# A selective-scan loop on one Trainium2 core: its order of work shifted by a few units, and the multiply by C done for two units at once

## The chip, the core and the metric

The kernel runs on one core of one Trainium2 chip. The core has five engines that run their own instruction streams and meet at semaphores: TensorE (PE; its weight loads are shown apart as PEld), VectorE (DVE), ScalarE (ACT), GpSimd (POOL) and SyncE (SP, which here issues the DMAs). The metric is the device time of one launch, in microseconds. The kernel before took 1730.82 us in the median of 3 runs (1728.37 to 1734.09).

## What is computed

Two attention and mixture-of-experts blocks stand ahead of and beside a stack of four Mamba layers; the change lies in the Mamba stack alone. For each of 4 layers and each of 4 parts of the batch (512 token columns in the kernel's layout), the reference does:

```python
xz = jnp.einsum('bld,ed->ble', x, in_w)
xi, z = jnp.split(xz, 2, axis=-1)
xc = silu(causal depthwise conv of 4 taps (xi) + cb)
dbc = jnp.einsum('bld,ed->ble', xc, xp_w)
dt, Bm, Cm = jnp.split(dbc, [DT_RANK, DT_RANK + D_STATE], axis=-1)
delta = jax.nn.softplus(jnp.einsum('blr,dr->bld', dt, dtw) + dtb)
A = -jnp.exp(A_log)
h = exp(delta * A) * h + (delta * u) * B        # the scan over the tokens
y = sum over the 16 states of h * C, + u * D
y = y * silu(z)
x = jnp.einsum('bld,od->blo', y, ow)
```

256 channels times 16 states give 4096 rows of a scan over the tokens, for each batch part. All of it is float32.

## The kernel before, in words

The Mamba stack is one block (from line 1333 on) whose engines each carry their own loop. The outermost loop runs over 4 layers `l`, inside it 4 steps `b`, one for each batch part. A step has 32 **units** (`UN`), numbered p: 128 scan rows each (32 channels times 4 states). Every fourth unit (p = 3, 7, 11, ...) is of kind DIRECT, the others are "main" units of three state groups k = 0, 1, 2, with eight units g = 0 to 7 in each group; so k = 0 fills p = 0 to 9, k = 1 p = 10 to 20, k = 2 p = 21 to 30.

For a unit the engines do this, each in its own turn:

- PE (`input_of`, lines 1638 to 1651) puts the scan's input into one of three PSUM banks `dbx`: four transposes of `scaled` for a main unit (L1650), one matmul with `spread` for a DIRECT unit (L1647). With three banks, unit p waits until the scan of unit p-3 has ended.
- ACT (`decay`, L1810) makes exp(dt * A) into a ring of five buffers (`DR`). The ring starts again with unit 0 in buffer 0 although 32 is no multiple of 5, so that unit 0 of a step needs the scan of unit 30, and unit 1 the scan of unit 31.
- DVE (`scan`, L1918) runs the scan into `hs`, a ring of eight (`HR`). For a DIRECT unit it first multiplies the bank by B (`times_b`, L1908).
- POOL (`weigh`, L1535) multiplies `hs` by C into `hcm` (ring of eight) or, for DIRECT units, `hck` (ring of four).
- PE (`fold_quad`, L1667) sums four such products into `y_bank`, eight times in a step, each time when the fourth of them is there.

Between the units each engine does the rest of the step, partly for the next one, n = b+1, at places that the code fixes by the unit's number (v for PE, w for ACT, u for DVE, p for POOL). PE: `z` at v = 0 and 2, `x_proj` at 3, `turn_b` at 6, `dt_proj` at 7 and 8, `start_y` at 10 and 11, `turn_du` at 18 and 19, `out_proj` of the step before at 22 (both halves), and `xi`, the convolution as four shifted matmuls for each half of the channels, with two taps at each of v = 24, 25, 27 and 28 (L1585). ACT: after the decay of unit 0 `silu_xi`, `silu_z` and two loads of function tables (L1737, L1743, L1821); then `copy_dbc`, `copy_bt`, `abs_and_relu` and `softplus`, `scale_by_b` for the groups 2 and 0, `copy_dut` in two halves, `copy_out`. DVE: `gate_y` after u = 4, `make_dt` and `make_du` after u = 12 to 15, and in layer 0 `mix` after u = 9. POOL: `scale_by_b` for group 1 (16 instructions a step: three after each of p = 27 to 31 and one after p = 0), in step b = 2 four `make_tap`, and in the steps 1 and 2 of layer 0 eight gathers by indirect DMA. SP stores and reads back the rows of B, C (`spread_direct`, `spread_c`) and dt (`spread_dt`), always in the same order.

The PSUM banks `slot` 0, 1 and 2 are shared by these side jobs (xi, z, x_proj, the transposes, dt, duT, out), so that each waits until the last reader of its bank is through. Ahead of the first step a prologue does the same jobs once for batch part 0, and `xi` for part 1. The four places where the order stands on PE are these lines of `step`:

```python
if v == 22:
    out_proj(l, b - 1)
...
if v in (24, 25, 27, 28):
    xi(l, b + 2, (v - 24) // 3, (0, 1) if v in (24, 27) else (2, 3))
```

## Time and profile before

| what | value |
|---|---|
| median of 3 runs | 1730.82 us (1728.37 to 1734.09) |
| the profiled execution | 1734.24 us, its span 1732.5 us |
| busy, of the span | PE 1307.1 us (75%), DVE 1186.3 (68%), ACT 1059.3 (61%), POOL 1006.6 (58%) |
| the Mamba stack | from about 748 us to 1716 us of the span |
| first scan of it starts, last ends | 787.9 us, 1703.5 us |

The page sums over the whole launch; the stretch of the Mamba stack is read in windows and in the timeline, engine by engine. "[4.42 <-ACT decay L1810]" behind an instruction says that its engine stood idle for 4.42 us before it and what ended that. An x4 behind a row merges four instructions that follow one another; a float32 matmul counts as two. Instructions of one engine overlap a little at their ends, so their pitch (start to start) is shorter than their duration, and it is the pitch that a sum of times needs.

### The profile page before, as it was taken

How to read it: one execution, taken by the hardware profiler on the slowest of the kernel's cores; microseconds unless marked ns; L12 is line 12 of the kernel's file. 1: busy time of each engine (PE TensorE's matmuls, PEld its weight loads, DVE VectorE, ACT ScalarE, POOL GpSimd, SP SyncE). 2: the span in 40 equal slices, each digit the busy share in tenths (PEclk: the TensorE clock that was granted, in tenths of full speed). 3: DMA queues.
4: the chain of work that ended last, by engine and by line, in shares of the span. 5: the costliest groups of instructions: out<-in, count | busy, mean ns of one | idle time of the engine just before them, and what ended most of it. 6: DMA issues, size and time to landing. Idle time of an engine off the chain costs nothing. (4 is left out here: it accounts for less than half of the span.)

```text
span 1732.5 us, 23857 instructions
## 1 busy us (share of the span) xinstructions
PE 1307.1 (75%) x6419; PEld 641.4 (37%) x6419; DVE 1186.3 (68%) x1664; ACT 1059.3 (61%) x1846; POOL 1006.6 (58%) x1092
## 2 busy tenths in 40 slices
PE   5213388898931799967977888898888989898884
PEld 2113033333431455633433334343443434343431
DVE  4786367686766422215888788878888778877884
ACT  2210378797811122346877779877798778777782
POOL 1642310110152530054988978898899888888894
PEclk9655589998965799987998999999999999999998
DMA  1110231321201301442332234313341233323331
GB/s 53 37 37 11 91 109 64 100 79 61 91 26 39 134 12 33 122 108 76 75 79 71 48 73 112 79 38 83 87 112 52 62 77 94 82 55 78 87 92 54
DMA packets 86612, 124.39 MB, mean 72 GB/s; under 512 B 16946, under 2 KB 43440, under 8 KB 86112
## 3 DMA queue, kind: packets, MB, share of 16 engines
q1 hardware_dynamic: 79680, 104.65, 23.0%
q0 software_dynamic: 6816, 18.42, 3.5%
q8 instruction: 44, 0.72, 0.2%
q14 instruction: 72, 0.59, 0.1%
HBM read 100.27 MB, written 24.31 MB: 72 GB/s over the span
## 5 line engine op out<-in xcount | busy, mean ns | idle before, releaser
L1918 DVE TENSOR_TENSOR_SCAN hs<-decay,dbx 128x512 f32<-128x512 f32 x512 | 592.3, 1203 | 100.7 <-ACT decay L1810 91.5
L1535 POOL TENSOR_TENSOR hcm<-hs,Cc 128x512 f32<-128x512 f32 x384 | 488.8, 1286 | 110.3 <-DVE hs L1918 106.8
L1810 ACT ACTIVATE decay<-dtr,a_cur 128x512 f32<-128x512 f32 x512 | 355.6, 714 | 145.3 <-DVE hs L1918 136.4
L1650 PE MATMUL dbx<-ident_sb,scaled 128*128 128x128 f32 x1536 | 242.5, 289 | 98.6 <-DVE hs L1918 95.2
L1650 PEld LDWEIGHTS dbx<-ident_sb,scaled 128*128 128x128 f32 x1536 | 176.5, 145 | 314.3 <-DVE hs L1918 240.5
L1790 ACT ACTIVATE scaled<-duT,BT 128x256 f32<-128x256 f32 x528 | 236.0, 497 | 0.1
L1535 POOL TENSOR_TENSOR hck<-hs,Cc 128x512 f32<-128x512 f32 x128 | 168.0, 1312 | 19.1 <-PE y_bank L1667 11.8
L1647 PE MATMUL dbx<-du,spread_sb 128*128 128x512 f32 x256 | 154.9, 690 | 11.0 <-DVE hs L1918 11.0
L1908 DVE TENSOR_TENSOR dbx<-dbx,Bb 128x512 f32<-128x512 f32 x128 | 88.6, 692 | 78.4 <-PE dbx L1647 77.3
L1585 PE MATMUL slot<-XT,w_tap 128*128 128x512 f32 (+3 forms) x288 | 138.4, 608 | 4.5 <-PEq L1063 3.7
L758 ACT ACTIVATE ex<-tt 128x1024 f32<-128x1024 f32 x128 | 136.8, 1069 | 4.2 <-DVE tt L843 3.5
L1517 POOL TENSOR_SCALAR scaled<-duT,BT 128x256 f32<-128x256 f32 x271 | 125.9, 480 | 8.7 <-PE dbx L1650 7.9
L1667 PE MATMUL y_bank<-hcm,fold_sb 128*32 128x512 f32 x768 | 108.0, 636 | 12.2 <-POOL hcm L1535 12.2
L842 DVE TENSOR_TENSOR tt<-bank_l,gt 128x512 f32<-128x512 f32 x128 | 87.6, 685 | 38.1 <-PE bank_l L667 34.5
L752 ACT ACTIVATE gt<-bank_d,dgh 128x512 f32<-128x512 f32 x128 | 89.0, 699 | 28.8 <-PE bank_d L661 28.8
L600 POOL CAST weight_rows<-w_row 128x1 uint32 (+1 forms) x26 | 4.9, 188 | 168.8 <-PE bank_e L685 168.8
L843 DVE SCALAR_TENSOR_TENSOR tt<-bank_l,gt 128x512 f32<-128x512 f32 x128 | 87.2, 681 | 0.0
L699 PE MATMUL bank_pv<-ex,v_head 128*32 128x512 f32 x512 | 76.0, 675 | 2.6 <-DVE ybig L832 2.6
L1502 POOL MEMSET w_dt<- 40x256 f32 x1 | 0.3, 306 | 124.5 <-POOLq L1063 124.5
L1585 PEld LDWEIGHTS slot<-XT,w_tap 128*128 128x128 f32 x288 | 52.3, 196 | 52.5 <-issue 52.5
L1647 PEld LDWEIGHTS dbx<-du,spread_sb 128*128 128x128 f32 x256 | 44.2, 205 | 63.5 <-DVE hs L1918 46.6
L661 PE MATMUL bank_d<-q_stack,k_stack 112*128 112x512 bf16 x128 | 54.3, 429 | 12.4 <-DMA k_stack<-qk_parts 7.8
(320 smaller groups left out, 2055.9 us busy)
## 6 DMA issues: line engine op xcount, KB each, us to landing
dtr<-dt_turn SPq DMA_DIRECT2D x68, 512.0 KB, 8.4
Cc<-bc_turn SPq DMA_DIRECT2D x268, 64.0 KB, 2.1
dt_turn<-dt SPq DMA_DIRECT2D x17, 512.0 KB, 2.8
Bb<-bc_turn SPq DMA_DIRECT2D x68, 64.0 KB, 2.1
conv_row<-in_conv_row SPq DMA_DIRECT2D x5, 512.0 KB, 3.8
w_rg<-in_w_rg SPq DMA_DIRECT2D x8, 256.0 KB, 2.8
w_ru<-in_w_ru SPq DMA_DIRECT2D x8, 256.0 KB, 3.0
w_rd<-in_w_rd SPq DMA_DIRECT2D x8, 256.0 KB, 3.9
```

The lines of the kernel that those rows point to most:

```text
L752: nc.scalar.activation(gt[:, st % RING, :], bank_d[st % 2][:, :], ACT.Tanh, scale=dgh[:, st // 16:st // 16 + 1]).then_inc(s_G, 1)
L758: nc.scalar.activation(ex[:, (st // 4) % 2, st % 4, :, :], tt[:, st % RING, :, :], ACT.Exp).then_inc(s_E, 1)
L1517: nc.gpsimd.tensor_scalar(scaled[:, (n + 1) % 2, kk, :, j, :], duT[:, n % 2, kk, :].rearrange("p (g c) -> p g c", c=32), BT[:, n % 2, kk, ...
L1535: nc.gpsimd.tensor_tensor(dst, hs[:, p % HR, :], rows, ALU.mult).then_inc(s_hc, 1)
L1585: last = mm(slot[h][:, d:512], w_tap[:, 3 - d, P * h:P * h + P], XT[:, n % 4, 0:512 - d], start=(d == 0), stop=(d == 3))
L1647: mm(dbx[p % 3][:, :], spread[:, g % 4, :], du[:, b % 2, g // 4, :], start=True, stop=True).then_inc(s_bx, 1)
L1650: last = nc.tensor.transpose(dbx[p % 3][:, P * kk:P * kk + P], scaled[:, (b + k) % 2, kk, g, :, :].rearrange("p j c -> p (j c)"), ident[:, :])
L1667: last = mm(y_bank[h][32 * q:32 * q + 32, :], fold[:, :], src, start=False, stop=((k, h) in ((DIRECT - 1, 0), (DIRECT, 1))), tile_position ...
L1790: nc.scalar.activation(scaled[:, (n + k) % 2, kk, :, j, :], duT[:, n % 2, kk, :].rearrange("p (g c) -> p g c", c=32), ACT.Copy, scale=BT[: ...
L1810: nc.scalar.activation(dec[:, p % DR, :], dtr[:, b % 2, g, :], ACT.Exp, scale=a_cur[:, 4 * g + k:4 * g + k + 1]).then_inc(s_dec, 1)
L1908: TT(dbx[p % 3][:, :], dbx[p % 3][:, :], Bb[:, b % 2, :], ALU.mult).then_inc(s_mul, 1)
L1918: nc.vector.tensor_tensor_scan(hs[:, p % HR, :], dec[:, p % DR, :], dbx[p % 3][:, :], 0.0, ALU.mult, ALU.add).then_inc(s_sc, 1)
```

## The change

- **POOL, C.** Main units are weighed in pairs of one state group (g = 0 and 1, 2 and 3, ...) in one instruction of 1024 columns, issued at the second unit's place; the C row is read twice by a broadcast. DIRECT units are weighed alone as before. A scan that reuses an `hs` buffer now waits for the pair (`hc_after`).
- **POOL, B.** The 16 `scale_by_b` go from three after each of p = 27 to 31 to two after each of p = 28 to 31 and 0 to 3.
- **DVE.** `times_b` of a DIRECT unit stands right before the scan of that unit (u % 4 == 3), not one scan earlier. `gate_y` moves from u = 4 to 7.
- **PE.** `xi` is cut into single taps at v = 19, 22, 23, 24 and 25, 27, 28, 29. `out_proj` moves from 22 to 13 and 14, one half each; `x_proj` is one half at 3 and one at 4; `z` comes at 0 and 1 in the other order of halves; `turn_du` from 18, 19 to 16, 17; the last two folds of the step before from 4, 5 to 5, 7; `dt_proj` from 7, 8 to 8, 9.
- **ACT.** `silu_z`, Abs and `copy_dut` each work on two banks in one instruction of 1024 columns (the `slot` banks become one tensor). The bias of dt comes in by a 41st row of `w_dt` against a row of ones in `dbc`; Relu falls away, and DVE's `make_dt` takes max(x, 0) in its addition. `scale_by_b` of group 2 goes to w = 13 to 20, that of group 0 starts at 22; `copy_out` moves from 25 to 16.
- **Prologue.** `xi` of part 1 goes to the `y_bank` banks and, with its Silu and the z of part 0, stands ahead of the first step; half of the first 16 `scale_by_b` of group 0 are DVE's, and POOL does 8 of its own ahead of the first step; SP sends dt out ahead of the three C rows.

The core of the diff (semaphore counts that only follow from it are left out):

```diff
-            slot = [st5.enter_context(nc.psum_tensor(f"slot{i}", [P, 512], fp32)) for i in range(3)]
+            slots = st5.enter_context(nc.psum_tensor("slots", [P, 3, 512], fp32))
+            slot = [slots[:, i, :] for i in range(3)]
...
+            weighed = lambda k, g: hc_after[place[k, g]]
+            hc_after = {}
+            for p, (k, g) in enumerate(units):
+                if k == DIRECT:
+                    hc_after[p] = p + 1
+                elif g % 2 == 1:
+                    hc_after[p] = hc_after[place[k, g - 1]] = p + 1
...
+                        sp.dma_start(w_dt[40:41, :].rearrange("o (h p) -> o h p", p=P), one(A["pre_cols"])[:, :, 2:4].rearrange("o p h -> o h p"), allow_slow_non_contiguous=True).then_inc(s_wpre, 16)
...
@@ -1524,15 +1533,15 @@
                             wait(pool, s_fk, at(l, b, 2, g // 4))
                             if g == 0:
                                 pool.wait_ge(s_c3[b % 2], by_parity(l, b, 128))
-                            dst, rows = hck[:, g % KR, :], Cc[:, 3 + b % 2, :]
+                            nc.gpsimd.tensor_tensor(hck[:, g % KR, :], hs[:, p % HR, :], Cc[:, 3 + b % 2, :], ALU.mult).then_inc(s_hc, 1)
                         else:
-                            m = order_in_main[k, g]
-                            if m % 4 == 0:
+                            m, q = order_in_main[k, g], place[k, g - 1]
+                            if m % 4 == 1:
                                 wait(pool, s_fm, at(l, b, 6, m // 4 - 1))
-                            if g == 0:
+                            if g == 1:
                                 pool.wait_ge(s_cb[k], at(l, b, 64, 64))
-                            dst, rows = hcm[:, m % MR, :], Cc[:, k, :]
-                        nc.gpsimd.tensor_tensor(dst, hs[:, p % HR, :], rows, ALU.mult).then_inc(s_hc, 1)
+                            nc.gpsimd.tensor_tensor(hcm[:, (m - 1) % MR:m % MR + 1, :], hs[:, q % HR:p % HR + 1:p - q, :],
+                                                    Cc[:, k:k + 1, :].broadcast_to([P, 2, 512]), ALU.mult).then_inc(s_hc, 2)
...
-                            weigh(l, b, p)
-                            if p == 0:
-                                scale_by_b(l, b, 15)
-                            if p >= 27:
-                                for x in range(3 * (p - 27), 3 * (p - 27) + 3):
+                            if units[p][0] == DIRECT or units[p][1] % 2 == 1:
+                                weigh(l, b, p)
+                            if p < 4:
+                                for x in (8 + 2 * p, 9 + 2 * p):
+                                    scale_by_b(l, b, x)
+                            if p >= 28:
+                                for x in (2 * (p - 28), 2 * (p - 28) + 1):
                                     scale_by_b(l, b + 1, x)
...
-                            if v == 0:
-                                z(l, b, 0)
-                            if v == 2:
-                                z(l, b, 1)
-                            if v == 3:
-                                x_proj(l, n)
-                            if not first(l, b):
-                                if v == 4:
-                                    fold_quad(l, b - 1, 2, 1)
-                                if v == 5:
-                                    fold_quad(l, b - 1, DIRECT, 1)
-                                if v == 22:
-                                    out_proj(l, b - 1)
+                            if v in (0, 1) and not first(l, b):
+                                z(l, b, 1 - v)
+                            if v in (3, 4):
+                                x_proj(l, n, v - 3)
                             if v == 6:
                                 turn_b(l, n)
-                            if v in (7, 8):
-                                dt_proj(l, n, v - 7)
+                            if v in (8, 9):
+                                dt_proj(l, n, v - 8)
+                            if not first(l, b):
+                                if v == 5:
+                                    fold_quad(l, b - 1, 2, 1)
+                                if v == 7:
+                                    fold_quad(l, b - 1, DIRECT, 1)
+                                if v in (13, 14):
+                                    out_proj(l, b - 1, v - 13)
                             if v in (10, 11):
                                 start_y(l, b, v - 10)
                             if v == 12:
                                 fold_quad(l, b, 0, 0)
                             if v == 15:
                                 fold_quad(l, b, 0, 1)
-                            if v in (18, 19):
-                                turn_du(l, n, v - 18)
+                            if v in (16, 17):
+                                turn_du(l, n, v - 16)
                             if v == 20:
                                 fold_quad(l, b, 1, 0)
                             if v == 21:
                                 fold_quad(l, b, DIRECT, 0)
-                            if v in (24, 25, 27, 28):
-                                xi(l, b + 2, (v - 24) // 3, (0, 1) if v in (24, 27) else (2, 3))
+                            if v in (19, 22, 23, 24):
+                                tap = (19, 22, 23, 24).index(v)
+                                xi(l, b + 2, 0, (tap,))
+                            if v in (25, 27, 28, 29):
+                                tap = (25, 27, 28, 29).index(v)
+                                xi(l, b + 2, 1, (tap,))
                             if v == 26:
                                 fold_quad(l, b, 1, 1)
                             if v == 31:
                                 fold_quad(l, b, 2, 0)
...
-                    x_proj(0, 0)
+                        xi(0, 0, h, every)
...
                         dt_proj(0, 0, h)
...
-                    for h in range(2):
-                        xi(0, 1, h, (0, 1, 2, 3))
+                    xi(0, 1, 1, every, y_bank)
+                    for h in (1, 0):
+                        z(0, 0, h)
...
                         wait(act, s_op, at(l, b, 1, -1))
-                        for h in range(2):
-                            act.wait_ge(s_z, at(l, b, 2, h + 1))
-                            nc.scalar.activation(zs[:, b % 2, h, :], slot[2 if h == 0 else 0][:, :], ACT.Silu).then_inc(s_zs, 1)
+                        act.wait_ge(s_z, at(l, b, 2, 2))
+                        nc.scalar.activation(zs[:, b % 2, :, :], slots[:, 0:3:2, :], ACT.Silu).then_inc(s_zs, 1)
...
+                        nc.scalar.activation(dt[:, :, :], slots[:, 0:2, :], ACT.Abs).then_inc(s_ab, 1)
+
+                    def exp_dt(l, n):
+                        act.wait_ge(s_ab, at(l, n, 2, 1))
                         nc.scalar.activation(dt[:, :, :], dt[:, :, :], ACT.Exp, scale=-1.0).then_inc(s_ab, 1)
...
-                            if w == 0:
+                            if w == 0 and not first(l, b):
                                 silu_xi(l, n)
                                 silu_z(l, b)
...
-                            if w == 8:
+                            if w == 7:
                                 copy_bt(l, n)
-                            if w in (10, 11):
-                                abs_and_relu(l, n, w - 10)
+                            if w == 10:
+                                abs_dt(l, n)
+                            if w == 11:
+                                exp_dt(l, n)
                             if w == 12:
-                                softplus(l, n)
-                            if 14 <= w < 22:
-                                for x in (2 * (w - 14), 2 * (w - 14) + 1):
+                                log_dt(l, n)
+                            if w in last_scales:
+                                for x in last_scales[w]:
                                     scale_by_b(l, b, 2, x)
-                            if w in (21, 22):
-                                copy_dut(l, n, w - 21)
-                            if 23 <= w < 31:
-                                for x in (2 * (w - 23), 2 * (w - 23) + 1):
+                            if w == 16 and not first(l, b):
+                                copy_out(l, b - 1)
+                            if w == 19:
+                                copy_dut(l, n)
+                            if 22 <= w < 30:
+                                for x in (2 * (w - 22), 2 * (w - 22) + 1):
                                     scale_by_b(l, n, 0, x)
-                            if w == 25 and not first(l, b):
-                                copy_out(l, b - 1)
-
+
...
+                    copy_dut(0, 0)
+                    for x in range(8):
                         scale_by_b(0, 0, 0, x)
+                    silu_xi(0, 1, y_bank)
+                    silu_z(0, 0)
+                    act.preload_act_table_set("natural_log_exp_and_others")
...
                 def _(dve):
+                    nc.vector.memset(dbc[32:41, :], 1.0).then_inc(s_one, 1)
...
-                        TT(dt[:, h, :], slot[h][:, :], dt[:, h, :], ALU.add).then_inc(s_dt, 1)
+                        nc.vector.scalar_tensor_tensor(dt[:, h, :], slot[h][:, :], 0.0, dt[:, h, :], ALU.max, ALU.add).then_inc(s_dt, 1)
...
-                        wait(dve, s_hc, at(l, b, UN, p - HR + 1))
+                        wait(dve, s_hc, at(l, b, UN, hc_after[p - HR] if p >= HR else hc_after[p - HR + UN] - UN))
...
-                            if u % 4 == 2:
+                            if u % 4 == 3:
                                 times_b(l, b, u // 4)
                             scan(l, b, u)
-                            if u == 4 and not first(l, b):
+                            if u == 7 and not first(l, b):
...
+                    dve.wait_ge(s_dut, 1)
+                    for x in range(8, 16):
+                        nc.vector.tensor_scalar(scaled[:, 0, x // 4, :, x % 4, :], duT[:, 0, x // 4, :].rearrange("p (g c) -> p g c", c=32),
+                                                BT[:, 0, x // 4, x % 4:x % 4 + 1], 1.0, ALU.mult, ALU.mult).then_inc(s_k[0], 1)
```

Three places as the instruction streams show them. First PE in step 1 of layer 0, around the end of the out projection and the first taps; `dbx` banks are inputs of units, `slot` the side jobs (L1650 and L1647 inputs, L1585 taps, L1667 folds, L1635 the out projection). Before, from v = 22 to 25:

```order
L1650 MATMUL dbx1<-ident_sb,scaled 128x128 x4
L1635 MATMUL slot2<-zs,w_out 128x512 x2
L1647 MATMUL dbx2<-du,spread_sb 128x512
L1650 MATMUL dbx0<-ident_sb,scaled 128x128 x4
L1585 MATMUL slot0<-XT,w_tap 128x512
L1585 MATMUL slot0<-XT,w_tap 128x511
L1650 MATMUL dbx1<-ident_sb,scaled 128x128 x4
L1585 MATMUL slot0<-XT,w_tap 128x510
L1585 MATMUL slot0<-XT,w_tap 128x509
```

The same place now, v = 22 to 25 (L1663 and L1660 inputs, L1597 taps):

```order
L1663 MATMUL dbx1<-ident_sb,scaled 128x128 x4
L1597 MATMUL slots<-XT,w_tap 128x511
L1660 MATMUL dbx2<-du,spread_sb 128x512
L1597 MATMUL slots<-XT,w_tap 128x510
L1663 MATMUL dbx0<-ident_sb,scaled 128x128 x4
L1597 MATMUL slots<-XT,w_tap 128x509
L1663 MATMUL dbx1<-ident_sb,scaled 128x128 x4
L1597 MATMUL slots<-XT,w_tap 128x512
```

Between two inputs there is now one tap where there were two, or the whole out projection; the first tap (512 columns) has gone ahead to v = 19, and the out projection to 13 and 14.

DVE in the same step, from unit 17 on. Before, and now:

```order
L1918 SCALAR_TENSOR_TENSOR hs<-decay,dbx 128x512 x2
L1908 TENSOR_TENSOR dbx<-dbx,Bb 128x512
L1918 SCALAR_TENSOR_TENSOR hs<-decay,dbx 128x512 x4
L1908 TENSOR_TENSOR dbx<-dbx,Bb 128x512
L1918 SCALAR_TENSOR_TENSOR hs<-decay,dbx 128x512 x4
```

```order
L1940 SCALAR_TENSOR_TENSOR hs<-decay,dbx 128x512 x3
L1930 TENSOR_TENSOR dbx<-dbx,Bb 128x512
L1940 SCALAR_TENSOR_TENSOR hs<-decay,dbx 128x512 x4
L1930 TENSOR_TENSOR dbx<-dbx,Bb 128x512
L1940 SCALAR_TENSOR_TENSOR hs<-decay,dbx 128x512 x4
```

The multiply by B follows one scan later, and the scan right behind it is now the one that reads its result.

POOL over the border of two steps. Before, from p = 27 to p = 2 of the next step:

```order
L1535 TENSOR_TENSOR hck<-hs,Cc 128x512
L1517 TENSOR_SCALAR scaled<-duT,BT 128x8x32 x3
L1535 TENSOR_TENSOR hcm<-hs,Cc 128x512
L1517 TENSOR_SCALAR scaled<-duT,BT 128x8x32
L1535 TENSOR_TENSOR hcm<-hs,Cc 128x512 x2
```

Now, from p = 26 to p = 4 of the next step:

```order
L1543 TENSOR_TENSOR hcm<-hs,Cc 128x1024
L1526 TENSOR_SCALAR scaled<-duT,BT 128x8x32 x4
L1543 TENSOR_TENSOR hcm<-hs,Cc 128x1024
L1526 TENSOR_SCALAR scaled<-duT,BT 128x8x32 x2
L1536 TENSOR_TENSOR hck<-hs,Cc 128x512
L1526 TENSOR_SCALAR scaled<-duT,BT 128x8x32 x4
L1543 TENSOR_TENSOR hcm<-hs,Cc 128x1024
L1526 TENSOR_SCALAR scaled<-duT,BT 128x8x32 x4
```

The 16 scalings are spread over eight units instead of six, and a step has 12 products of 1024 columns and 8 of 512 where it had 32 of 512.

## Rows read from the trace of the kernel before

**Rows 1.** Windows, 1414:1471: length, busy PE, PEld, DVE, ACT, POOL, PE clock, DMA, GB/s.

```profile
1414.00:1471.00 57.00, 50.95 (x243) 23.09 (x242) 45.01 (x47) 45.93 (x84) 48.60 (x49) 0.94 0.30 73
```

**Rows 2.** Timeline, ACT: first table load of the steps 4 and 15.

```profile
1033.94 1.28 ACT L1737 ACT_TABLE_LOAD   x1
...
1648.94 1.28 ACT L1737 ACT_TABLE_LOAD   x1
```

**Rows 3.** Waits of DVE from 1072 to 1700 us: total us, times, longest.

```profile
DVE dbx L1908 <- PE dbx L1647: 60.2, 46, 2.9
DVE hs L1918 <- ACT decay L1810: 49.8, 14, 5.5
```

**Rows 4.** Timeline, ACT: a step's border, and Exp of 1024 columns (start, duration).

```profile
1422.12 0.72 ACT L1810 ACTIVATE decay<-dtr,a_cur 128x512 f32<-128x512 f32 x1 [4.87 <-DVE hs L1918]
...
1424.16 1.27 ACT L1737 ACTIVATE xc<-slot,pre_cols 128x512 f32<-128x512 f32 x2
...
1426.68 1.28 ACT L1821 ACT_TABLE_LOAD   x1
...
1441.02 1.05 ACT L1773 ACTIVATE dt<-dt 128x1024 f32<-128x1024 f32 x1
```

**Rows 5.** Timeline, DVE, one step.

```profile
1428.73 1.22 DVE L1918 TENSOR_TENSOR_SCAN hs<-decay,dbx 128x512 f32<-128x512 f32 x1 [4.42 <-ACT decay L1810]
...
1464.01 0.70 DVE L1908 TENSOR_TENSOR dbx<-dbx,Bb 128x512 f32<-128x512 f32 x1 [2.88 <-PE dbx L1647]
1464.62 4.54 DVE L1918 TENSOR_TENSOR_SCAN hs<-decay,dbx 128x512 f32<-128x512 f32 x4
1470.80 0.70 DVE L1908 TENSOR_TENSOR dbx<-dbx,Bb 128x512 f32<-128x512 f32 x1 [1.64 <-PE dbx L1647]
```

**Rows 6.** Timeline, PE: a fold at either clock, the out projection, an input, taps.

```profile
1441.72 1.06 PE L1659 MATMUL y_bank<-xc,d_diag 128*32 128x512 f32 x8
...
1457.07 1.94 PE L1667 MATMUL y_bank<-hcm,fold_sb 128*32 128x512 f32 x8
...
1461.23 1.88 PE L1635 MATMUL slot<-zs,w_out 128*128 128x512 f32 x4
1462.95 1.02 PE L1647 MATMUL dbx<-du,spread_sb 128*128 128x512 f32 x2
...
1465.97 0.60 PE L1650 MATMUL dbx<-ident_sb,scaled 128*128 128x128 f32 x4
1466.40 1.87 PE L1585 MATMUL slot<-XT,w_tap 128*128 128x510 f32 x4
```

**Rows 7.** Timeline, DVE, last stage: L1977 reads what L1974 wrote.

```profile
1722.58 0.68 DVE L1974 TENSOR_TENSOR GATE<-s_bank,GATE 128x512 f32<-128x512 f32 x1
...
1723.30 0.69 DVE L1977 TENSOR_TENSOR X<-X,GATE 128x512 f32<-128x512 f32 x1
```

**Rows 8.** POOL by form (count, busy us, mean ns), and L334 under a busy DVE.

```profile
L1535 POOL TENSOR_TENSOR hcm<-hs,Cc 128x512 f32<-128x512 f32 x384 | 488.8, 1286 | 110.3 <-DVE hs L1918 106.8 <-PE y_bank L1667 2.8
...
L1541 POOL TENSOR_TENSOR w_tap<-w_in,conv_row 128x256 f32<-128x256 f32 x16 | 11.7, 730 | 0.0
...
54.48 2.87 POOL L334 TENSOR_TENSOR sq<-qkv 128x1024 f32<-128x1024 f32 x1
```

**Rows 9.** Timeline, POOL: a product and three scalings.

```profile
1426.24 1.27 POOL L1535 TENSOR_TENSOR hcm<-hs,Cc 128x512 f32<-128x512 f32 x1
1427.48 1.40 POOL L1517 TENSOR_SCALAR scaled<-duT,BT 128x256 f32<-128x256 f32 x3
```

**Rows 10.** Timeline, prologue: the dt rows' way out and back, and the first scans.

```profile
771.55 0.39 SPq L1448 DMA_DIRECT2D dt_turn<-dt  x1
...
787.13 0.72 ACT L1810 ACTIVATE decay<-dtr,a_cur 128x512 f32<-128x512 f32 x1 [8.61 <-DMA dtr<-dt_turn]
...
794.68 1.22 DVE L1918 TENSOR_TENSOR_SCAN hs<-decay,dbx 128x512 f32<-128x512 f32 x1 [5.58 <-ACT decay L1810]
```

**Rows 11.** Timeline, DVE: the last gate, after the last scan.

```profile
1712.45 1.29 DVE L1890 TENSOR_TENSOR zs<-y_bank,zs 128x512 f32<-128x512 f32 x2 [8.90 <-issue]
```

153 lines of the change are left out of this document (75 added, 78 removed).

## The prediction, made before the changed kernel had run

> **What bounds the kernel now.** The launch is one long chain of stages; only the Mamba stack changes, and it holds 968 of the 1732.5 us. So I read windows first. In 57 us of its later layers no engine is full by the page's measure: PE 51.0 us, POOL 48.6, ACT 45.9, DVE 45.0 [rows 1]. When all are near 80 to 90% and none is full, the time goes where they wait for each other, and the next view is the waits of DVE, since its scans are the one thing that cannot be reordered.
>
> A step's length I take from ACT's first table load, once a step: steps 4 to 15 are (1648.94 - 1033.94)/11 = 55.9 us apart [rows 2]; the four of layer 0, with `mix` and the gathers, are longer. From 1072 to 1700 us, 11.2 steps, DVE waited 60.2 us for PE's L1647, always in the multiply by B of a DIRECT unit, and 49.8 us for `decay`: 5.4 and 4.45 us a step [rows 3]. So of 55.9 us DVE works about 46.0 (smaller idle times counted in).
>
> The timeline says what these two are. (a) At a step's border ACT makes the decay of unit 0 only when scan 30 has freed its buffer (1422.12), then loads a table, does four Silus, loads the other table, and comes to the decay of unit 1 at 1427.96 [rows 4]; DVE has run dry and stands 4.42 us [rows 5]. (b) The bank of a DIRECT unit p may be filled once scan p-3 has ended; its matmul takes 1.02 to 1.12 us and DVE wants it after one scan of 1.13 us (the pitch: 4.54/4). There is no slack, and anything that PE puts between two inputs shows. It puts the whole out projection ahead of unit 23: DVE waits 2.88 us. Taps by twos around 24 to 28: 1.64 us [rows 5, 6].
>
> **PE's budget** decides what (b) is worth. Four units take DVE 4 x 1.13 + 0.61 = 5.1 us. PE's four inputs take 3 x 0.45 to 0.6 + 1.0, about 2.5 us, so 2.6 us are left for side jobs in each group of four. A fold or `start_y` costs 1.0 us of pitch, a tap or half an out projection 0.86 (1.72 for the out projection, 1461.23 to 1462.95, and two taps show the same 1.87 as it does) [rows 6]. In v = 20 to 27 the kernel before has three folds, the out projection and six taps: 3.0 + 1.7 + 5.2 = 9.9 us against 5.2. The excess of 4.7 us is the 2.88 + 1.64 seen. The method reproduces the trace there.
>
> **The change, part by part** (times a step of layers 1 to 3 unless said).
>
> *Taps, out projection, multiply by B.* Now v = 20 to 27 hold three folds and five taps, 7.3 us against 5.2; the 2.1 us excess meets a new slack of one scan, 1.1 us, since the multiply by B comes one scan later, and the groups ahead (16 to 19: two `turn_du` and one tap, some 2.1 us) leave PE no debt. In v = 4 to 15 PE has about 11.5 us of side jobs against 7.8, but there DVE itself does six extra operations (two each of `gate_y`, `make_dt`, `make_du`, at 0.58, 3.5 us). I leave 0.6 us of waits out of 5.4: -4.8 us. PE's whole work does not shrink; at these pitches its 32 inputs and side jobs come to about 46.5 us, so it fits into 52, with little to spare.
>
> *The price of the later multiply.* The scan now reads what the instruction just ahead wrote. No row of the stack shows that. In the last stage a TT that depends on its predecessor starts 0.72 us after it [rows 7]; in the stack the scan behind a multiply that it does not need starts 0.61 us after it [rows 5]: +0.11 us, eight times, +0.9. Bounds: 0 (if the scan starts late anyway) to 0.2 each, 0 to 1.6 us. The Trainium skill (VectorE: DVE Perf Modes, "The DRAIN you can't avoid") says that a semaphore between Vector operations costs nothing extra; by it this term would be 0. The last-stage pair speaks against that, so I keep 0.9.
>
> *The border.* It stays, and gets a little longer. z of half 0 must wait for the first Silu of xi (it takes bank 0), which ends about 2.73 us after unit 0's decay began; its matmul takes 1.02. Before, ACT did one z Silu meanwhile; now a single one of 1024 columns starts after it and takes about as long as ACT's Exp of 1024 columns, 1.05 us. So the second table load starts some 4.9 us after the decay instead of 4.56 [rows 4]: +0.4.
>
> *ACT elsewhere.* Relu gone, Abs and `copy_dut` merged: about 2 us less work, on an engine on which DVE waited elsewhere for under 0.5 us a step. I cost it at nothing; the cover is the decay ring, five deep. `copy_dbc` and Abs come later because PE's `x_proj` and `dt_proj` do, by one unit; the ring carries that too.
>
> *POOL.* A product takes 1.27 us, pitch 1.24; three scalings 1.40, pitch 1.36 [rows 9]. The 1024-column product is not in the trace with these operands. 256 columns of the same kind take 0.73 us and 512 take 1.286, so 0.556 for 256 more, and 1024 would take 1.286 + 2 x 0.556 = 2.4 us. A 1024-column product of an earlier stage, beside a DVE at work on two SBUF operands, took 2.87 [rows 8]. Bounds 2.3 and 2.9; I take 2.4, since the scans beside it read one operand from PSUM and the 512-column rows there are at their low value. POOL's step is then 12 x 2.36 + 8 x 1.24 + 16 x 0.455 = 45.5 us where it was 47.0; at 2.87 it is 51.5. POOL waits about 1 us for the fold of the first four DIRECT products, which stays at v = 21. So POOL is no bound in layers 1 to 3. The pair is finished later than its first half was, but a scan reuses its buffer only eight units on. Worth: nothing there. In layer 0, steps 1 and 2 have 8 gathers of about 1.3 us on POOL and step 2 the four taps: 45.5 + 10.4 + 2.9 = 59 us where it was 60.3; there it counts.
>
> *Sum of a step*: -4.8 + 0.9 + 0.4 = -3.5, and with the 0.4 us of small waits for decay and issue that taking the load off ACT and PE should remove, -3.9: 52.0 us. Twelve steps: **-47 us**. Layer 0 I give -3 a step, as POOL and `mix` hold part of it: **-12**.
>
> *Prologue.* dt goes out to DRAM at 771.55 because SP is still issuing C rows, and the first decay waits until 787.13 for the way back [rows 10]. Now SP sends it as soon as it is made, near 767.7: -3.8. Silu, z and both table loads are done while the rows travel, so that the 5.58 us hole after scan 0 [rows 10] is gone. Against this, a load of 256 single elements for the bias row joins the first weights: 0 to 1 us, taken as 0.2. Sum **-9**. If C rows in the same queues slow the dt rows, 3 us of it go.
>
> *End.* From the last scan's end, 1703.55, to the last gate DVE waits 8.90 us for POOL and the folds [rows 11]; POOL has then five triples of scalings between products, now four pairs, and two pairs ahead of the last product: about 7 x 0.45, less half a product for the pairing: **-2.5**.
>
> Sum: 47 + 12 + 9 + 2.5 = 70.5 us off the profiled execution's own 1734.2 us: 1664. The profiled execution lies 3.4 us above the median of the runs, 1730.8, so for a median I say **1660 us**. About 0.3%, 5 us, is what a measurement of this kernel can tell from no change.
>
> **Rivals.**
> 1. *PE becomes the bound by its clock.* The granted clock in these 57 us is 0.94 of full [rows 1]: near 1457 a fold takes 1.94 us instead of 1.06 [rows 6], so the engine is at the 1.2 GHz level there, after a stretch in which it had waited for `du`. The new order moves `turn_du` two units earlier, ahead of the second `du`, which puts a wait of some 1.4 us at v = 17. The missing 6% are 6.8 us at half clock, 3.4 us of work lost. If that stays, and falls where PE has no slack, more than half of it shows, 2 us a step: 54: layers 1 to 3 give -23, layer 0 -6, ends -11, total -40: 1691. For: PE has only 5 us to spare. Against: PE stands idle less than before. Chance 0.22.
> 2. *Better than the sum*: the scan behind the multiply costs nothing extra (the rule named above), and the low-clock stretch vanishes with PE's idle time, so that no wait for PE is left. Then 0.9 + 0.6 more a step, 16 steps, 24 us: 1636. The rule alone gives 1646. Chance 0.13.
> 3. *The waits only move.* PE's excess in v = 4 to 15 shows on DVE, say 1.3 us in each group, and the border grows by 1: a step gains nothing, only prologue and end count: 1719. Chance 0.06.
> 4. *Slower: POOL's pairs are dear.* If a 1024-column product with a strided `hs` pair and a broadcast C row runs at a slower rate than a plain one, POOL becomes the bound, and DVE waits for `hs` buffers. POOL's step without pairs is 9.9 + 7.3 + 1.0 = 18.2 us; it reaches 55.9 at 3.14 us a pair, and from there the kernel is slower. At 3.5 us a step is 60.2: 16 x 4.3 - 11 = 58 us more: 1789. For: no row has this form. Against: a broadcast operand is in nearly all forms that a plain one is, and even the row under contention is 2.87. Chance 0.03.
>
> **How the numbers follow.** The forecast has 0.56, and its own range, from the bounds of the dependence (0 to 1.6 us), the pair and the prologue, is 1646 to 1680. The range reaches to rival 1 and to rival 2: 1636 to 1694; it leaves out rivals 3 and 4 and their neighbours, about one in ten, and as much again for what I have not seen. Faster by over 0.3%: the forecast, rivals 1 and 2 and nearly all of 3, 0.93. Slower: rival 4 and an unseen wait, 0.04. The same: 0.03.
>
> **What would show it.** Steps 52 us apart at ACT's table load. DVE's waits for L1660 (the old L1647) near zero, its wait for decay once a step and 4.5 to 5 us. Multiply to scan 0.72 us apart at the eight DIRECT units. POOL's 1024-column rows at 2.4 us. Scan 0 starting near 784 us and scan 1 right behind. If POOL's pairs are over 2.9 us, or DVE's waits for `hs` buffers appear, the POOL part is wrong; if waits for PE stay above 2 us a step, the PE budget or its clock is; if the hole at the border is under 4 us, I have misread what unit 1's decay waits for.

## The result: 0.6% faster, and 60 us short of the forecast

| | before | after |
|---|---|---|
| median | 1729.85 us (20 runs) | 1719.98 us (1701.73 to 1736.61, 20 runs) |
| ratio | | 0.9941 (95%: 0.9923 to 0.9959) |
| profiled execution, its span | 1734.24, 1732.5 us | 1714.21, 1712.4 us |
| DVE busy, whole launch | 1186.3 us | 1226.5 us |
| POOL busy, whole launch | 1006.6 us | 975.4 us |

The forecast was 1660 us with a range of 1636 to 1694, so 1720 lies outside it, though it is faster, as was forecast. The two profiled executions differ by 20 us, the medians by 10: single runs of this kernel scatter by a per cent. To see where the 20 us lie I cut each launch at ACT's first table load of a step, as [rows 2] did:

| piece of the span, us | before | after | forecast |
|---|---|---|---|
| to the border load of step 1 | 847.13 | 837.62 (-9.5) | -9, and -3 for step 0 |
| steps 1 to 3 (layer 0) | 186.81 | 189.30 (+2.5) | -9 |
| steps 4 to 14, a step | 55.91 | 54.42 (-16.4 in all) | 52.0 (-43) |
| the last step and the end | 83.56 | 86.84 (+3.3) | -6.4 |

The prologue with the first step came within 3 us of the forecast. The other steps did not. ACT's first table load in steps 4 and 15 of the kernel after (start, duration, engine, line):

```profile
1026.92 1.28 ACT L1757 ACT_TABLE_LOAD   x1
...
1625.56 1.28 ACT L1757 ACT_TABLE_LOAD   x1
```

**The waits fell, most of the way.** DVE's waits from 1060 to 1680 us (11.4 steps) in the kernel after: total us, times, longest.

```profile
DVE hs L1940 <- ACT decay L1827: 43.3, 12, 4.2
DVE dbx L1930 <- PE dbx L1660: 17.1, 29, 0.8
DVE hs L1940 <- PE dbx L1663: 6.1, 11, 2.1
DVE hs L1940 <- issue: 3.7, 6, 1.9
DVE hs L1940 <- POOL hcm L1543: 2.4, 7, 0.4
```

The wait at the multiply by B fell from 5.4 us a step [rows 3] to 1.5, the border's is 3.8. All waits together are 6.4 us a step where they were some 10 and where the forecast came to about 5. Yet a step is only 1.5 us shorter, so DVE's own work must have grown, and the windows say so. The stretch of [rows 1] in the kernel after:

```profile
1414.00:1471.00 57.00, 48.45 (x245) 21.62 (x245) 48.86 (x48) 46.60 (x84) 49.70 (x43) 1.00 0.35 89
```

DVE is busy for 48.9 us there and was for 45.0 (part of that is that 57 us now hold more of a step: a whole one, from table load to table load, has 47.2 us at 1409.87 and had 44.8 at 1422.86). PE's granted clock is full in this stretch; it isn't in others, as e4 will show. The groups of DVE's instructions tell which ones grew (x count, busy us, mean ns), first of before, then of after, 760 to 1720 us:

```profile
L1883 DVE TENSOR_TENSOR du<-dt,xc 128x512 f32<-128x512 f32 x34 | 32.8, 966 | 0.0
L1897 DVE SCALAR_TENSOR_TENSOR GATE<-back,share,GATE 128x128 f32<-128x128 f32 x32 | 23.7, 802 | 0.1
```

```profile
L1905 DVE TENSOR_TENSOR du<-dt,xc 128x512 f32<-128x512 f32 x34 | 52.6, 1550 | 0.0
L1919 DVE SCALAR_TENSOR_TENSOR GATE<-back,share,GATE 128x128 f32<-128x128 f32 x32 | 28.5, 951 | 0.1
```

The same 34 `du`, with the same operands, cost 1550 ns each instead of 966. The timeline shows how. DVE and then POOL in one step of the kernel after:

```profile
1435.60 1.21 DVE L1940 TENSOR_TENSOR_SCAN hs<-decay,dbx 128x512 f32<-128x512 f32 x1
1436.72 2.28 DVE L1905 TENSOR_TENSOR du<-dt,xc 128x512 f32<-128x512 f32 x1
1438.93 0.69 DVE L1930 TENSOR_TENSOR dbx<-dbx,Bb 128x512 f32<-128x512 f32 x1
```

```profile
1434.85 1.29 POOL L1536 TENSOR_TENSOR hck<-hs,Cc 128x512 f32<-128x512 f32 x1
1436.08 5.14 POOL L1543 TENSOR_TENSOR hcm<-hs,Cc 128x1024 f32<-128x1024 f32 x2
1441.19 1.72 POOL L1536 TENSOR_TENSOR hck<-hs,Cc 128x512 f32<-128x512 f32 x1
```

`du` begins 0.64 us after a pair did (the row merges two; at 2.38 us the first ends near 1438.45) and lasts to 1439.00, 0.55 us beyond that pair. In another step it lasts 4.59 us (1107.79 to 1112.38), through two pairs (1107.15 to 1111.83). And with POOL quiet, in the kernel before, DVE and POOL:

```profile
821.90 0.67 DVE L1883 TENSOR_TENSOR du<-dt,xc 128x512 f32<-128x512 f32 x1
```

```profile
822.06 1.63 POOL L1535 TENSOR_TENSOR hcm<-hs,Cc 128x512 f32<-128x512 f32 x1 [1.03 <-DVE hs L1918]
```

There POOL had run dry, `du` was first and took 0.67 us, and it is POOL's product that is stretched, from 1.27 to 1.63 us. The scans and the multiply by B, with one input in SBUF and one in PSUM, show no such thing: beside the same POOL instructions they keep their 1.21 and 0.69 us. Only `du` and `mix` read two SBUF tensors in the loop. With 0.67 us for a free `du` and 0.29 for a free `mix` (found below) the hold makes up 10.0 + 14.4 = 24.4 us of DVE's busy time in the kernel before and 29.8 + 19.2 = 49.0 after: 25 us more, on the engine whose time the forecast had added up.

The Trainium skill (SBUF — State Buffer, "Who interferes with whom") has this rule: a DVE instruction with two SBUF inputs contends with a GpSimd instruction that reads SBUF, whoever issues first gets the shared ports for the whole instruction, and the other fully blocks. The traces agree, with 0.67 against 2.28 us. They show more than it says in one respect, the 4.59 us through two instructions.

### The profile page after: what moved, and what is told of

The parts are those of the page before. It is cut to its first block and busy times, and to the rows that moved or that the text cites. A ratio compares the mean times of both kernels' runs of the same rounds, so it can differ in the third digit from the quotient of the medians.

```text
span 1712.4 us, 23568 instructions
## 1 busy us (share of the span) xinstructions
PE 1307.6 (76%) x6419; PEld 638.9 (37%) x6419; DVE 1226.5 (72%) x1673; ACT 1018.5 (59%) x1754; POOL 975.4 (57%) x893
## 5 line engine op out<-in xcount | busy, mean ns | idle before, releaser
L1543 POOL TENSOR_TENSOR hcm<-hs,Cc 128x1024 f32<-128x1024 f32 x192 | 456.3, 2385 | 31.8 <-DVE hs L1940 27.2
L1827 ACT ACTIVATE decay<-dtr,a_cur 128x512 f32<-128x512 f32 x512 | 350.5, 711 | 69.9 <-DVE hs L1940 66.2
L1663 PEld LDWEIGHTS dbx<-ident_sb,scaled 128*128 128x128 f32 x1536 | 183.8, 147 | 315.3 <-DVE hs L1940 185.9
L1663 PE MATMUL dbx<-ident_sb,scaled 128*128 128x128 f32 x1536 | 253.9, 290 | 55.8 <-DVE hs L1940 54.1
L1807 ACT ACTIVATE scaled<-duT,BT 128x256 f32<-128x256 f32 x520 | 229.4, 496 | 2.0 <-PE dbx L1663 1.9
L1660 PE MATMUL dbx<-du,spread_sb 128*128 128x512 f32 x256 | 146.1, 654 | 8.8 <-DVE hs L1940 8.8
L1597 PE MATMUL slots<-XT,w_tap 128*128 128x512 f32 (+3 forms) x272 | 143.9, 616 | 3.7 <-PEq L1063 3.7
L1526 POOL TENSOR_SCALAR scaled<-duT,BT 128x256 f32<-128x256 f32 x264 | 122.0, 480 | 1.4 <-issue 1.4
L1312 DVE TENSOR_TENSOR hid<-sil,u_bank 128x512 f32<-128x512 f32 x32 | 21.9, 687 | 59.4 <-ACT sil L1222 59.0
L1660 PEld LDWEIGHTS dbx<-du,spread_sb 128*128 128x128 f32 x256 | 43.7, 202 | 55.6 <-issue 27.5
```

The lines of the kernel that those rows point to most:

```text
L1526: nc.gpsimd.tensor_scalar(scaled[:, (n + 1) % 2, kk, :, j, :], duT[:, n % 2, kk, :].rearrange("p (g c) -> p g c", c=32), BT[:, n % 2, kk, ...
L1543: nc.gpsimd.tensor_tensor(hcm[:, (m - 1) % MR:m % MR + 1, :], hs[:, q % HR:p % HR + 1:p - q, :], Cc[:, k:k + 1, :].broadcast_to([P, 2, 512 ...
L1597: last = mm(dst[h][:, d:512], w_tap[:, 3 - d, P * h:P * h + P], XT[:, n % 4, 0:512 - d], start=(d == 0), stop=(d == 3))
L1660: mm(dbx[p % 3][:, :], spread[:, g % 4, :], du[:, b % 2, g // 4, :], start=True, stop=True).then_inc(s_bx, 1)
L1663: last = nc.tensor.transpose(dbx[p % 3][:, P * kk:P * kk + P], scaled[:, (b + k) % 2, kk, g, :, :].rearrange("p j c -> p (j c)"), ident[:, :])
L1807: nc.scalar.activation(scaled[:, (n + k) % 2, kk, :, j, :], duT[:, n % 2, kk, :].rearrange("p (g c) -> p g c", c=32), ACT.Copy, scale=BT[: ...
```

## The experiments

Each was profiled and timed in five rounds beside the kernel before; ratios are to that kernel on the same chip. Theory H is the hold, as read above.

| kernel | median us | ratio, 95% | to step 1 | steps 1-3 | a step of 4-14 | rest |
|---|---|---|---|---|---|---|
| e0_after_again | 1716.4 | 0.9925 (0.9897-0.9954) | 835.6 | 188.2 | 55.18 | 83.9 |
| e1_no_pairs | 1735.3 | 1.0042 (1.0026-1.0059) | 835.8 | 185.5 | 56.55 | 83.8 |
| e2_before_pairs | 1738.8 | 1.0067 (1.0044-1.0090) | 846.6 | 187.8 | 55.97 | 88.1 |
| e3_b_early | 1749.0 | 1.0127 (1.0104-1.0150) | 837.4 | 196.5 | 56.58 | 84.4 |
| e4_du_psum | 1676.9 | 0.9700 (0.9679-0.9721) | 837.2 | 186.5 | 51.87 | 80.5 |
| e5_du_pool | 1735.1 | 0.9865 (0.9837-0.9893) | 863.6 | 191.5 | 53.98 | 85.0 |
| e6_du_gap | 1725.6 | 0.9809 (0.9781-0.9837) | 860.8 | 187.7 | 54.02 | 81.6 |
| e8_pool_mix | 1736.4 | 0.9867 (0.9840-0.9893) | 856.4 | 192.1 | 54.30 | 84.8 |
| e9_fold_early | 1720.5 | 0.9779 (0.9751-0.9808) | 863.9 | 185.3 | 53.54 | 80.6 |
| e10_gap_fold | 1679.1 | 0.9713 (0.9688-0.9739) | 837.5 | 186.2 | 52.00 | 82.6 |
| e11_du_bank | 1696.3 | 0.9806 (0.9780-0.9831) | 840.7 | 187.1 | 53.10 | 83.7 |
| e12_bank_fold | 1696.0 | 0.9807 (0.9786-0.9827) | 839.3 | 184.9 | 52.97 | 83.0 |
| e13_mix_gap | 1667.6 | 0.9645 (0.9621-0.9668) | 833.7 | 178.8 | 52.13 | 82.1 |
| e14_ring_on | 1654.5 | 0.9571 (0.9547-0.9595) | 834.3 | 185.6 | 50.17 | 79.8 |
| e15_ring_mix | 1644.5 | 0.9513 (0.9489-0.9537) | 834.6 | 178.1 | 50.22 | 79.9 |
| e16_mix_quarter | 1671.1 | 0.9673 (0.9647-0.9698) | 832.5 | 181.3 | 51.96 | 80.5 |

The last four columns are of each profiled execution. e5, e6, e8 and e9 ran on a chip where the stages ahead of the stack took some 25 us more (first scan 811.80 in e9 against 785.90) and the kernel before took 1761.5 us; their steps compare, their totals only by the ratio.

### One part alone

**e4_du_psum**: `du` reads the PSUM bank, so its softplus is left out.

```diff
-TT(du[:, n % 2, h, :], dt[:, h, :], xc[:, n % 2, h, :], ALU.mult)
+TT(du[:, n % 2, h, :], slot[h][:, :], xc[:, n % 2, h, :], ALU.mult)
```

> The kernel after, with du's first input read from the PSUM bank (dt before the softplus, which is left out of du) instead of from SBUF: the same shape and cost for DVE, but only one of its inputs lies in SBUF. Theory H: du takes 0.67 us or a little more at all 34 places (busy 23 us in place of 53), and the launch gets up to 30 us shorter: 1690 to 1702. Theory P: du takes 0.67 too, but the waits for PE take the place: 1713 to 1722. Rival to both, that du is slow for another reason than two SBUF inputs: du stays at 1.5 us and the time at 1720.

```profile
L1905 DVE TENSOR_TENSOR du<-slots,xc 128x512 f32<-128x512 f32 x34 | 22.6, 667 | 0.0
```

All 34 take 667 ns, and the launch is about 40 us shorter, more than the 30 of `du` itself: PE's wait for `du` (35.0 us in the kernel after) falls to 11.6. Steps 4 to 14 are 51.87 us apart; the forecast said 52.0. Theory P is out, and so is another reason for the slow `du`: only the place of one input changed.

**e4 also frees PE's clock.** Steps 4 to 14 as one stretch, in the kernel before, in the kernel after and in e4 (us, then busy PE, PEld, DVE, ACT, POOL, the granted clock, DMA):

```profile
1033.94:1648.94 615.00, 540.93 (x2641) 247.77 (x2640) 502.29 (x507) 497.55 (x903) 533.54 (x541) 0.95 0.32 77
1026.92:1625.56 598.64, 535.88 (x2642) 242.15 (x2641) 525.75 (x507) 472.55 (x847) 514.78 (x409) 0.96 0.33 79
1023.70:1594.32 570.62, 522.09 (x2642) 233.29 (x2641) 500.49 (x507) 471.11 (x847) 506.01 (x409) 0.99 0.35 83
```

DVE works 45.7 us a step before, 47.8 after and 45.5 in e4, and the clock rises too. It is uneven from step to step. In the kernel after, five of these eleven steps have the clock at 1.00 throughout and take 52.2 to 53.1 us, from table load to table load; the other six, at 0.91 to 0.97, take 54.0 to 58.6 (two of them also have a `du` of 4.59 us). Two steps with the same place in their layer (b = 2) and the same two `du` (0.87 and 2.22 us), and in each PE at its wait for `du`:

```profile
1136.94:1191.92 54.98, 49.73 (x243) 22.77 (x241) 47.42 (x47) 42.69 (x76) 48.84 (x41) 0.94 0.32 75
1357.63:1409.87 52.24, 46.99 (x243) 21.15 (x241) 46.94 (x47) 42.68 (x76) 48.85 (x41) 1.00 0.34 79
```

```profile
1170.32 1.09 PE L1637 MATMUL slots<-ident_sb,du 128*128 128x128 f32 x4 [2.81 <-DVE du L1905]
1389.49 0.63 PE L1637 MATMUL slots<-ident_sb,du 128*128 128x128 f32 x4 [2.81 <-DVE du L1905]
```

PE had stood for 2.81 us both times. In the first step the granted clock is at its lower level, 0.50, from 1169.9 to 1173.3, and the same transposes take 1.09 us instead of 0.63; with a second such stretch, at 1146.0, behind PE's wait for a scan at the border, that step is 2.7 us longer. Why the clock fell in one and not in the other is open. In steps 4 to 14 of the kernel after ten such stretches last 44 us in all (61 us in the kernel before), five of them at PE's wait for `du` or just behind it; in e4 there are two (7 us) and none at that wait. My estimate from these rows: of the 28 us that e4 saves in steps 4 to 14, some 10 are the shorter `du` at full clock (52.5 us a step against 51.6), and the other 18 lie in the six steps with a low clock. No run keeps the hold and gives the clock back, so the two are not parted further.

**e1_no_pairs**: products by C one unit at a time again, the rest of after stays.

```diff
-if units[p][0] == DIRECT or units[p][1] % 2 == 1:
-    weigh(l, b, p)
+weigh(l, b, p)
```

> The kernel after, with POOL's product by C one unit at a time (512 columns) again; all else stays. Theory H (DVE is held by POOL): a DVE operation with two SBUF inputs (du, and in layer 0 mix) stands while POOL's product runs, and the 2.38 us pairs made that longer: du takes 1550 ns in the mean where it took 966 before and 0.67 when free, and du and mix together lost about 45 us where they had lost 21. With single products du's mean falls below 1.1 us, some 20 us come back, less what POOL itself loses (1.4 us a step, where it is not the bound nothing): 1700 us, 1692 to 1712. Theory P (PE has no time left): DVE's long du only fills time in which PE would be late; du gets shorter, DVE's waits for PE grow by as much, and the time stays at 1715 to 1725.

Missed, and it corrected the theory. `du` got worse, not better:

```profile
L1900 DVE TENSOR_TENSOR du<-dt,xc 128x512 f32<-128x512 f32 x34 | 65.0, 1913 | 0.0
```

DVE's `du` and POOL in one step:

```profile
1442.92 4.06 DVE L1900 TENSOR_TENSOR du<-dt,xc 128x512 f32<-128x512 f32 x1
```

```profile
1442.68 3.75 POOL L1540 TENSOR_TENSOR hcm<-hs,Cc 128x512 f32<-128x512 f32 x3
```

It is held through three products in a row, to 0.55 us after their end. So the length of one instruction isn't what counts, but how far POOL is behind at that moment: with work queued it can go from one instruction to the next without DVE getting in. The pairs save POOL time and so shorten the queue; within the new order they are worth 15 to 19 us.

**e2_before_pairs**: the kernel before with the pairing alone.

```diff
-weigh(l, b, p)
+if units[p][0] == DIRECT or units[p][1] % 2 == 1:
+    weigh(l, b, p)
```

> The kernel before, with the pairing of POOL's products alone. Theory H: du's mean rises from 966 ns to 1.3 to 1.6 us and mix's from 802 to about 950, 15 to 25 us more of DVE, of which the waits for PE around 13 to 15 may hide a little: 1738 to 1755. Theory P: DVE had 10 us a step of waits in the kernel before, the longer du goes into them, and POOL gets 1.4 us a step shorter: 1722 to 1733. A third theory, that pairs help POOL where it is the bound (layer 0): 5 to 10 us faster in layer 0 alone.

As theory H had it at its lower end: 0.7% slower, `du` 1367 ns (`mix` 854, less than the 950 expected). In steps 4 to 14 nothing shows (55.97), since the longer `du` goes into waits for PE that were there (57.0 us before, 51.7 now); what the profile shows of the loss is mostly in the last step and the end. The same edit thus costs about 10 us in one order and saves 15 or more in the other.

**e3_b_early**: the multiply by B back one scan earlier.

```diff
-if u % 4 == 3:
+if u % 4 == 2:
     times_b(l, b, u // 4)
```

> The kernel after, with the multiply by B back one scan earlier (after u % 4 == 2). If the later multiply bought slack of a scan, as the prediction has it: the wait for PE at the multiply rises from 1.5 us a step to 3 to 5, the pitch from multiply to scan falls from 0.70-0.79 back to 0.61 (1.0 us a step), net 1 to 2.5 us a step slower: 1735 to 1760. Rival: the waits had gone because PE's side jobs were spread, and the later multiply only costs its dependence: 10 to 16 us faster, 1704 to 1712.

29 to 33 us slower than after. The wait at the multiply is 48.8 us again (17.1 in after), so the slack of one scan is real, and the largest of the parts that a run took out alone: without it the new order is 1.3% slower than the kernel before. The price on the other side, from multiply to scan, in the kernel after:

```profile
1418.47 0.67 DVE L1930 TENSOR_TENSOR dbx<-dbx,Bb 128x512 f32<-128x512 f32 x1
1419.18 1.22 DVE L1940 TENSOR_TENSOR_SCAN hs<-decay,dbx 128x512 f32<-128x512 f32 x1
```

0.71 us in this row, 0.70 to 0.80 over all 128 of them and 0.74 in the mean, against 0.61 in [rows 5] (0.58 to 0.61, in e3 too): a little more than the 0.11 forecast from [rows 7].

### Taking POOL's queue away

**Why is POOL behind** at unit 14? Its waits from 1060 to 1680 us in the kernel after, the main one, and the place in a step:

```profile
POOL hck L1536 <- PE y_bank L1680: 61.8, 22, 4.2
```

```profile
1424.48 1.26 POOL L1536 TENSOR_TENSOR hck<-hs,Cc 128x512 f32<-128x512 f32 x1 [2.62 <-PE y_bank L1680]
```

The first DIRECT product waits for the last fold of the step before, which the change moved from v = 5 to 7; from there POOL runs without a break into unit 14.

**e9_fold_early** and **e6_du_gap**:

```diff
# e9: the last two folds of the step before
-if v == 5: fold_quad(l, b - 1, 2, 1)
-if v == 7: fold_quad(l, b - 1, DIRECT, 1)
+if v == 4: fold_quad(l, b - 1, 2, 1)
+if v == 5: fold_quad(l, b - 1, DIRECT, 1)
# e6: DVE makes both du after scan 14; POOL, ahead of weigh(l, b, 14):
+pool.wait_ge(s_dun, at(l, b + 1, 2, 2))
```

> The kernel after, with the last two folds of the step before back at v = 4 and 5 (they had gone to 5 and 7). POOL stood 2.62 us a step for the second one, at the first DIRECT product, and ran its products back to back from there to unit 13, which is the backlog that held du. Theory H with this cause of the backlog: POOL's wait there falls under 1 us, du's mean from 1.55 to about 1.0, 10 to 20 us faster: 1700 to 1712. Rival: PE's denser v = 4 to 6 puts the fold's 1.0 us on DVE's multiply at unit 7, and the backlog comes from the pairs: 1718 to 1728.

> The kernel after, with both du of a step after scan 14, and POOL waiting for them ahead of unit 14's product, so that POOL stands still while they run; nothing else moves. If du is held only by a POOL instruction already running or queued, it falls to 0.67 us wherever POOL has caught up by then, else it waits for POOL's backlog alone and no longer: du's mean 0.8 to 1.4. Theory H: 1690 to 1708; POOL loses up to 1.5 us a step. Rival: POOL's backlog at that place is so long (products back to back from unit 4 on) that du is held until the wait is reached, 2 to 4 us: 1715 to 1730.

e9: POOL's waits for these folds fall from 61.8 to 17.5 us, `du` to 1106 ns, a step to 53.54 us. By its ratio it comes to 1692 us where the kernel before takes 1729.85, more than was expected. e6: `du` stays at 1508 ns, as the rival said, yet a step is 0.4 to 1.2 us shorter than in the two profiles of after, and the ratio gives 1697, theory H's time. From the load of step 1 to the end, e9 takes 854.8 us, e6 863.5, and after 874.8 and 879.1; as after itself did not run on that chip, I trust these more than the ratios.

**e10_gap_fold** has both edits, e0_after_again is after on the same chip.

> The kernel after once more, unchanged, as the measure for the other three of this group on the same chip. Every theory: 0.994 of before, 0.992 to 0.996, if the ratio does not depend on the chip; the group before this one, on a chip where the kernel before took 1761 us, gave ratios that look up to 1% better than the first group's, and without this run it can't be said how much of that is the chip.

> The kernel after with both edits that shorten the hold: the last two folds back at v = 4 and 5, and both du after scan 14 with POOL waiting for them. The first alone brought du's mean from 1.55 to 1.11, the second alone to 1.51 with POOL's waits for du. Theory H (the hold is POOL's backlog at that place): with no backlog the wait is reached in time, du's mean 0.67 to 0.85, 8 to 15 us under the better of the two alone: ratio 0.968 to 0.975. Rival: POOL loses by its wait what DVE wins, 1.5 us a step: within 4 us of the kernel with the folds early.

DVE and POOL in e10:

```profile
1415.85 1.26 DVE L1907 TENSOR_TENSOR du<-dt,xc 128x512 f32<-128x512 f32 x2
```

```profile
1412.76 2.37 POOL L1543 TENSOR_TENSOR hcm<-hs,Cc 128x1024 f32<-128x1024 f32 x1
1417.33 2.35 POOL L1543 TENSOR_TENSOR hcm<-hs,Cc 128x1024 f32<-128x1024 f32 x1 [2.21 <-DVE du L1907]
```

Two `du` in 1.26 us, POOL standing beside them for 2.21 us that it can spare, a mean of 798 ns over all `du`, steps 52.00 us apart with the granted clock at 0.99, 37 us under after with the same computation. Neither edit does it alone: a wait that POOL reaches late holds nothing back.

**Other ways to free du.** e5_du_pool lets POOL make `du` (two products ahead of unit 14's); e8_pool_mix adds `mix` after unit 0. e11_du_bank writes dt into its bank, `du` reads it there, and ACT copies dt out for the DMA (DVE now makes dt and `du` of one half, then of the other, and PE's `turn_du` waits for the copy); e12_bank_fold adds the early folds.

```diff
# e5, on POOL; e8 also: mix(b) at u == 0
+nc.gpsimd.tensor_tensor(du[:, n % 2, h, :], dt[:, h, :], xc[:, n % 2, h, :], ALU.mult)
# e11
-nc.vector.scalar_tensor_tensor(dt[:, h, :], slot[h][:, :], 0.0, dt[:, h, :], ALU.max, ALU.add)
+nc.vector.scalar_tensor_tensor(slot[h][:, :], slot[h][:, :], 0.0, dt[:, h, :], ALU.max, ALU.add)
+nc.scalar.activation(dt[:, h, :], slot[h][:, :], ACT.Copy)
```

> The kernel after, with du made by POOL (two products of 512 columns ahead of unit 14's) instead of by DVE; the result is the reference's. Reading the two inputs from PSUM took 43 us off, so the hold of du is what the forecast had missed; the question is how much of it a kernel with the right result can have. DVE loses two operations a step (1.17 us) and the whole hold; POOL gets 2 x 1.25 us more, 48 of 52 us. Theory H: 1675 to 1688. Rival (POOL becomes the bound, as it stands 2.6 us a step for the fold of the DIRECT products and 2.5 for two more products): the wait comes back as PE's for du at turn_du and as DVE's for hs buffers: 1695 to 1715.

> As e5_du_pool, and in layer 0 mix goes from after unit 9 to after unit 0, into the border where DVE waits 4.2 us for the second decay anyhow. mix takes 28.5 us in its 4 x 8 instructions, 951 ns each, as it too reads two SBUF tensors. Theory H: 3 to 4 us less in each of three or four steps of layer 0, so 8 to 15 us under e5_du_pool. Rival: layer 0 is bound by POOL and its gathers, and mix is held by the scalings that POOL runs at the border: within 3 us of e5_du_pool.

> The kernel after, with dt written into its PSUM bank instead of to SBUF, du reading it there (so that one of its two inputs lies in SBUF), and ACT copying dt out for the DMA, half by half after du; the result is the reference's. Theory H: du 0.67 us everywhere, as in the run that left the softplus out (43 us under after), less what ACT's two copies of 0.7 us and the later dt cost, 0 to 0.7 us a step, and 1.5 us in the prologue: 30 to 42 us under after, ratio 0.970 to 0.976. Rival: ACT, which waits 3.3 us a step for PE's dt already, becomes late with duT and the scalings by B: 5 to 20 us under after.

> As e11_du_bank, with the last two folds back at v = 4 and 5 too. Theory H: with du out of POOL's way POOL's backlog is harmless but for layer 0's mix, so the folds' place is worth 0 to 6 us more. Rival: that POOL stands for the fold is a cost by itself (POOL is near its bound in layer 0): 8 to 15 us under e11_du_bank. Third: PE's denser v = 4 to 6 costs DVE up to 0.5 us a step, and the run is up to 8 us slower than e11_du_bank.

e5: the rival was right. The ratio gives 1706 us, and a step is 53.98: PE's wait for `du` hardly falls (28.7 us, 35.0 in after; e4, which had put one of the two inputs in PSUM, had 11.6), and DVE's waits for decay and for issue grow from 43.3 and 3.7 us to 55.5 and 19.4. e8 brings nothing on top (`mix` 889 ns, against 966 in e5). e11: `du` is 667 ns everywhere, but a step is 53.1 us: PE waits 17.7 us for ACT's copy and DVE 18.5 us for the inputs (6.1 in after); half of the expected gain. e12's folds add 0.

### Layer 0 and the border

**e13_mix_gap** lets POOL wait for `mix` too; **e16_mix_quarter** leaves out three of four of mix's instructions; **e14_ring_on** lets the decay ring run on across steps; **e15_ring_mix** has e13 and e14 together.

```diff
# e13, ahead of weigh(l, b, 9) in layer 0
+pool.wait_ge(s_fin, 2 * b + 2)
# e14
-dec[:, p % DR, :]
+dec[:, (UN * b + p) % DR, :]
-if w == 0 and not first(l, b):
+if w == (1 if b == 0 else 2) and not first(l, b):
     silu_xi(l, n)
```

> e10_gap_fold, and in layer 0 POOL also waits for mix before the product at unit 9, so that mix does not run beside it. Theory H: mix's instructions fall from 832 ns to about 0.25 us each, and layer 0 gets 2 to 3 us a step shorter, 8 to 12 us in all: ratio 0.964 to 0.967. Rival (in steps 1 and 2 POOL runs without a break from the gathers to the next step's unit 12, so it is the bound and its wait costs as much): ratio 0.970 to 0.973, as e10_gap_fold.

> e10_gap_fold with three of four of mix's instructions left out (24 of 32, so that tokens of three tiles in four don't get their expert outputs): the hold by POOL's product stays, the work of 24 x 0.25 us goes. Theory H (the hold is most of mix's 26.6 us): 4 to 7 us faster, and the two instructions of a step that are left take over 1 us in the mean. Rival (mix's own instructions are slow, 0.8 us each): up to 19 us faster.

> e10_gap_fold with the decay ring running on over the border of two steps (unit p of step b in buffer (32b + p) mod 5; over a layer's border it slips by two), and the Silus after the decay of unit 2 (unit 1 in the first step of a layer) instead of unit 0. If the ring's new start is what makes DVE wait 4.2 us at the border: the wait falls to under 1 us in three of four steps and to 1 to 2 in the fourth, and of some 3.5 us a step PE and POOL (46 and 45 us a step) leave at least half: 25 to 45 us under e10_gap_fold, ratio 0.945 to 0.957. Rival: the wait moves to PE's z and x_proj, which need the Silus early, or to POOL, which has its 16 scalings there: within 10 us of e10_gap_fold.

> Both edits, the ring running on and POOL's wait for mix. If they add, the sum of the two gains, within 3 us. If POOL bounds layer 0, the second is worth nothing here.

`mix` in e13, eight instructions in one row, and in e16, the two of a step that are left as a group:

```profile
855.11 2.32 DVE L1923 SCALAR_TENSOR_TENSOR GATE<-back,share,GATE 128x128 f32<-128x128 f32 x8
```

```profile
L1922 DVE SCALAR_TENSOR_TENSOR GATE<-back,share,GATE 128x128 f32<-128x128 f32 x8 | 17.3, 2157 | 0.1
```

Free, eight take 2.32 us; held, each pair of them alone takes 4.3. Leaving out 24 of 32 gained 8 us, a little over the 4 to 7 expected; only letting POOL wait gained 11.6, with nothing left out. That the gathers make POOL the bound of layer 0, the rival, is refuted: steps 1 to 3 fell by 7.4 us though POOL's work was the same.

e14: DVE's waits for decay, 45.3 us in e10, are one of 0.4:

```profile
DVE dbx L1934 <- PE dbx L1664: 15.7, 24, 0.8
DVE hs L1944 <- POOL hck L1538: 8.9, 9, 1.0
...
DVE hs L1944 <- ACT decay L1831: 0.4, 1, 0.4
```

Yet a step is 1.8 us shorter, not 3.8, and the gain of 24.6 us is at the low edge of what was expected. `du` is at 1190 ns again: POOL had used the border's pause to catch up, and now is behind at unit 14. The two edits add up (1644.5 against 1642.9 for the sum). **e15_ring_mix** leaves nothing of the computation out, and beats the kernel after by some 4.2% and the one before by 4.9% (4.6 to 5.1).

## Why the prediction was wrong

Point by point, in its own order:

- **"So of 55.9 us DVE works about 46.0"** is the step that failed: I took this work as given and, but for the dependence, let only waits change. 24 us of the busy time in the kernel before were hold already: `du` had a mean of 966 ns, and steps at 0.67 beside steps at 4.02 us. The mean of a group with equal operands and unequal durations was there to be read. In the new order the work of steps 4 to 14 grew from 45.7 to 47.8 us a step: about 1.3 for longer `du` (1550 ns where it was 966 in the mean of all), the rest the dependence, for which the sum had 0.9. It had nothing for `du`. [rows 8] had the contention in it, but I read it as a price for POOL alone. With the hold gone (e4, e10) the step is 51.9 and 52.0 us. That this meets 52.0 to a tenth is partly luck: the 46.0 held 0.9 us a step of hold that e4 takes away too.
- **POOL.** A pair takes 2.385 us, 2.4 forecast. "POOL is no bound" was right, and the wrong question: POOL off the critical path still set how long DVE's `du` ran. "POOL waits about 1 us for the fold of the first four" missed the other wait, 2.62 us for the fold that went from v = 5 to 7, where POOL fell behind (e9).
- **Taps, out projection, multiply by B**: -4.8 forecast; the wait at the multiply fell by 3.9 us a step, and to 0.6 us, as forecast, only in the steps with the clock at 1.00. e3 shows that the later multiply carries most.
- **The dependence**: 0.11 forecast, 0.10 in the row above, 0.14 in the mean of all. It is not 0, so rival 2 falls.
- **The border**: on ACT it got longer as forecast, from the decay of unit 0 to that of unit 1 6.35 us (1409.12 to 1415.47) where it was 5.85. DVE's wait got shorter all the same, 4.17 us against 4.42: the multiply by B of unit 31 (0.7 us) now stands behind scan 30 and fills part of it, which the forecast left out. What unit 1's decay waits for, the ring and the Silus, was right (e14).
- **Prologue**: -9 forecast and -3 for the first step, -9.5 for both. Scan 0 starts at 785.90, not near 784, and dt left at 769.37 instead of 771.55, not at 767.7; the hole after scan 0 is gone.
- **Layer 0**: -12 forecast, nothing came; +2.5 in steps 1 to 3. I put it on POOL's gathers; e13 shows that the hold of `mix` is 7 us there.
- **End**: the last gate waits 6.88 us instead of 8.90, -2.0 where -2.5 was forecast; the last step as a whole gave it back.
- **Rivals.** Rival 1 (PE's clock) came in part: in six of the steps 4 to 14 low stretches stayed (0.91 to 0.97), and the mean step of 54.4 us is near its 54; the window of [rows 1] happens to be at 1.00. Half of its stretches lie where it said, at PE's wait for `du`, but that wait was 2.8 us and more and not 1.4, since `du` itself was held; e4 takes both away. Its reading of the kernel before was off: ahead of the low stretch at 1452.6 PE had waited for scans (1.31 and 1.06 us), not for `du`:

```profile
1451.65 0.66 PE L1650 MATMUL dbx<-ident_sb,scaled 128*128 128x128 f32 x4 [1.06 <-DVE hs L1918]
```

- Rival 3 gave 1719, the right number by a wrong mechanism: the waits did fall, and longer work and slow stretches of PE took the gain. The chances of the named cases add up to 1.00 and so left nothing for the unseen cause to which the text gives a tenth; such a cause came.

What stays open: why a hold ends after one POOL instruction at 1436.72 and after two at 1107.79, when `du` came 0.64 us behind POOL both times; and what lets the clock fall in some steps. Not tried: another place for `du` in e15, where 29 us of hold are left by the same count (`du` 39.4 - 22.8, `mix` 21.4 - 9.3).

## What to carry to other kernels

Look at an instruction's own duration, not only at what it waits for: the same form at 0.67 and at 4 us means that something outside holds it, and a wait view shows none of it. A DVE instruction with two SBUF inputs beside a busy POOL can last until POOL pauses; give it a pause (let POOL wait for it, at a place where POOL is not behind), or put one input in PSUM. A held instruction can cost on a third engine as well: PE waited for `du`, and five stretches of half clock began at or just behind that wait. So compare whole steps with their granted clock, not one window. What a piece of a change is worth depends on the order around it: the pairs cost about 10 us in the old one and saved 15 or more in the new.

## What the runs showed of the hardware

- The hold can span POOL instructions that follow one another without a pause: `du` of 0.67 us took 2.28 us behind one pair, 4.59 through two pairs, 4.06 through three single products, and in e0 7.42 through five instructions (from 1161.30), each time to about 0.55 us beyond the last one's end.
- It takes two SBUF inputs: with one in PSUM all 34 took 667 ns beside the same POOL. The scan, with one of each, kept 1.2 us in all kernels.
- In the other order it is POOL that is stretched, by the 0.36 us of 1.27 to 1.63.
- A POOL instruction of 1024 columns with a broadcast row and a strided pair took 2.385 us, 0.19 less than two of 512 at 1.286.
- At half granted clock the same four float32 transposes of 128 columns took 1.09 us instead of 0.63, after the same wait of PE of 2.81 us in both steps. With `du` free, the stretches of half clock in steps 4 to 14 went from 44 us to 7 (e4, e10).
